# A row copy one exponential sooner, and products of constants in three further gaps of the FFN's first tiles

## The reference, cut to what matters

```python
scores = jnp.einsum('bhqd,bhkd->bhqk', q, k) * scale      # 16 heads of 16
attn = jax.nn.softmax(scores, axis=-1)
msa = jnp.einsum('bhqk,bhkd->bhqd', attn, v)
...
gate = fp4_linear(x, w_gate)                              # 256 -> 704
y = fp4_linear(x, w_up)
h = jax.nn.silu(gate) * y
return fp4_linear(h, w_down)                              # fp4_linear quantises x and w in blocks of 16
```

## Time and profile before

| | us |
|---|---|
| three runs: median (lowest to highest) | 1751.27 (1739.05 to 1756.83) |
| the profiled execution, its own time | 1747.05 |
| its span, first to last instruction | 1745.3 |
| TensorE busy in the span | 1568.2 |
| VectorE busy | 1328.9 |
| ScalarE busy | 889.5 |
| GpSimd busy | 285.7 |

### The profile page before, as it was taken

The page is one execution under the profiler, slowest core; times in us unless marked ns, Lnnn a source line. Parts: engine busy times, 40 slices in busy tenths (PEclk is TensorE's granted clock), DMA queues, the critical chain, the costliest instruction groups (busy, mean ns, idle before and its releaser), DMA issues.

```text
span 1745.3 us, 28266 instructions
## 1 busy us (share of the span) xinstructions
PE 1568.2 (90%) x10646; PEld 940.9 (54%) x10646; DVE 1328.9 (76%) x2565; ACT 889.5 (51%) x1358; POOL 285.7 (16%) x383
## 2 busy tenths in 40 slices
PE   5977899996599999899999979999997999999895
PEld 1757899995243335565333557533335654333564
DVE  3585565542499988888998889899888889997686
ACT  1213354442357776144777624477772356778312
POOL 0053223222200030301003130100223010000120
PEclk8988999998699999899999989999999999999998
DMA  3127878775222220004222000322200022210000
GB/s 135 49 73 208 246 242 258 244 244 163 58 42 38 38 74 1 1 8 87 34 39 68 14 1 1 79 38 38 68 26 1 1 61 47 38 29 2 1 0 25
DMA packets 80306, 123.07 MB, mean 71 GB/s; under 512 B 13657, under 2 KB 55898, under 8 KB 80170
## 3 DMA queue, kind: packets, MB, share of 16 engines
q1 hardware_dynamic: 70794, 93.46, 20.7%
q0 software_dynamic: 9376, 27.80, 5.5%
HBM read 76.84 MB, written 18.61 MB: 55 GB/s over the span
## 4 chain that ended last, share of the span: by engine, by line
PE 71%; DVE 17%; issue 6%; ACT 3%; DMA 2%; POOL 1%; SPq 1%; ACTq 0%; DVEq 0%; POOLq 0%
PE PS L1065 13%; PE PS L1018 13%; PE PS L1176 7%; PE PS L943 7%; PE PS L931 6%; PE PS L1051 6%; DVE MX L1581 6%; PE PS L1186 5%; PE PS L988 3%; PE PS L1002 2%; PE PS L881 2%; PE PS L1135 1%; PE PS L1212 1%; DMA Pb<-W 1%; PE PS L920 1%
## 5 line engine op out<-in xcount | busy, mean ns | idle before, releaser
L1581 DVE TENSOR_REDUCE MX<-PS 128x1 f32<-128x512 f32 x1024 | 636.5, 683 | 70.1 <-PE PS L1018 69.2
L748 ACT ACTIVATE Pb<-PS 128x1024 f32<-128x1024 f32 x512 | 518.9, 1026 | 180.0 <-PE PS L1051 179.4
L1018 PE MATMUL PS<-Ks,Qs 48*128 48x512 f32 x1024 | 389.8, 455 | 35.0 <-ACT MR L741 28.8
L1051 PE MATMUL PS<-Qs,Ks 50*128 50x512 f32 x1024 | 360.4, 452 | 0.0
L1065 PE MATMUL PS<-Pb,V 128*32 128x256 f32 x4096 | 320.5, 390 | 0.5
L1018 PEld LDWEIGHTS PS<-Ks,Qs 48*128 48x128 f32 x1024 | 161.9, 184 | 243.7 <-DVE MX L1581 133.7
L1065 PEld LDWEIGHTS PS<-Pb,V 128*32 128x32 f32 x4096 | 83.8, 108 | 162.0 <-ACT Pb L748 87.1
L1051 PEld LDWEIGHTS PS<-Qs,Ks 50*128 50x128 f32 x1024 | 143.5, 185 | 24.4 <-ACT Pb L748 19.8
L943 PE MATMUL PS<-Pb,OT 128*128 128x256 f32 x624 | 141.0, 379 | 0.0
L931 PE MATMUL PS<-Ks,Qs 128*128 128x256 f32 x936 | 127.6, 294 | 8.0 <-DVE Ks L1461 8.0
L931 PEld LDWEIGHTS PS<-Ks,Qs 128*128 128x128 f32 x936 | 119.8, 197 | 10.5 <-DVE Ks L1461 9.4
(11 more groups left out here) (288 smaller groups left out, 1959.6 us busy)
## 6 DMA issues: line engine op xcount, KB each, us to landing
Pb<-W SPq DMA_DIRECT2D x78, 512.0 KB
y_slot<-V SPq DMA_DIRECT2D x39, 256.0 KB
Qs<-Qh SPq DMA_DIRECT2D x128, 64.0 KB, 2.3
Ks<-Kh SPq DMA_DIRECT2D x120, 64.0 KB, 2.3
V<-b SPq DMA_DIRECT2D x39, 128.0 KB
XT<-x_mid POOLq DMA_DIRECT2D x4, 1024.0 KB
out<-Pb POOLq DMA_DIRECT2D x4, 1024.0 KB, 6.8
OT<-xT SPq DMA_DIRECT2D x2, 1024.0 KB, 6.4
```

What stands on the lines that cost most here:

```text
L748: F["ex"].inc(act.activation(weights_of(n), PS[:, 2 * (n % 2):2 * (n % 2) + 2, :], ACT.Exp, scale=0.25))
L1018: F["slp"].inc(pe.matmul(PS[:, slot_bank(i), :], Qs[rows, p % NB, t * P:(t + 1) * P], Ks[rows, p % NB, kh * HALF:(kh + 1) * HALF], start=T ...
L1051: ins = pe.matmul(PS[:, 2 * (n % 2) + a, :], Ks[rows, p % NB, kt * P:(kt + 1) * P], Qs[rows, p % NB, qh * HALF:(qh + 1) * HALF], start=Tru ...
L1581: F["sld"].inc(dve.tensor_reduce(MX[:, p % 2, a, t, kh:kh + 1], PS[:, slot_bank(i), :], AX.X, ALU.max))
```

## The change

`turn_step` gives one step less for every unit from 1 to 15, so each copy of rows stands behind the exponential ahead of the one where it stood. TensorE's order in attention stays as it was. In the FFN the 36 products of the identity become 42, and three further groups are put in: 4 after the turns of x's tiles 0 and 1, 12 after the turn of tile 2 (ahead of `gate_up(1)`), and 12 after `gate_up(1)` (ahead of the turn of `HQ(0)`). The three further groups write bank 7.

```diff
             if u + 1 == NU:
-                return LAST + 1
-            return next(n for n in range(NU * KT) if ahead_of(n + 1) > UN * (u + 1) + LATER)
+                return LAST
+            return next(n for n in range(NU * KT) if ahead_of(n + 1) > UN * (u + 1) + LATER) - 1
...
-                for _ in range(36):
-                    pe.matmul(PS[:, 3, 0:P], ident[:, :], ident[:, :], start=True, stop=True)
+                def identities(n, bank):
+
+                    for _ in range(n):
+                        pe.matmul(PS[:, bank, 0:P], ident[:, :], ident[:, :], start=True, stop=True)
+
+                identities(42, 3)
...
                 F["trp"].inc(x_tile_turn(1, 4, D))
+                identities(4, 7)
                 gate_up(0)
                 F["trp"].inc(x_tile_turn(2, 5, 0))
+                identities(12, 7)
...
                     if t:
                         down(t - 1)
+                    else:
+                        identities(12, 7)
```

## The result

The kernel after takes 1733.0 us (median of 17 runs, 1719.34 to 1765.63) and the kernel before, beside it, 1756.56 us (17 runs, 1739.05 to 1771.09). The ratio is 0.9909, with a 95% interval of 0.988 to 0.9939: faster by 0.6 to 1.2%. The ratio goes by the fast executions alone, those within 1.5% of the fastest of their kernel, so it is not the quotient of the two medians, 0.9866. Forecast were 1711 us and a range of 1702 to 1729. The sign is right. The size is 16.0 us by the ratio and 23.6 by the medians, where 38 to 40 were forecast. A result within 1% had been given 0.07. The profiled execution took 1728.35 us, 18.7 us less than that of before.

What follows compares the result with a forecast made beforehand. The prediction took TensorE, busy 1568.2 of 1745.3 us, as the bound, so its idle places count. Copy 32 us and constants 6 us off 1747.05 give 1709, or 1713 from the median; forecast 1711 us, range 1702 to 1729.

Steps and rivals of the forecast that it cites:

- The copy's mechanism: In attention, the copy of rows starts one exponential sooner, so TensorE's score product no longer waits for its slot.
- Its size: Attention's gain from the sooner copy: 0.67 us in each of 52 units, bounds 26 to 35 us, 32 us taken.
- second rival: In attention, VectorE's reduction soon holds the score product instead and half the gain is lost: 1725 us; chance 0.13.
- first rival: In attention, the copy waits for the turned product and holds ScalarE's exponential: slower, 1762 us; chance 0.06.
- The constants: In the FFN's head, added products keep TensorE's clock up, shortening each sequence's third gate_up to 4.74 us: 6 us taken.
- The sum: Whole kernel: 1747.05 - 32 - 6 = 1709 us; from the runs' median 1713; 1711 us taken.
- third rival: In the FFN's head, the clock falls despite the fill; the last twelve products run at 1.2 GHz: 1726 us; chance 0.11.

Runs made afterwards that it cites:

- after again: The changed kernel, unaltered, run for a second profile on chip 12: 1760.61 us, with no ratio on record.
- chip 15: Chip without stalls; there the unaltered kernels were run again: after 1697.99 us (ratio 0.9812), before 1732.02 us (1.0009).
- The two kernels made for this question: The kernel after with the copy sooner only in units 1 to 11: 1702.74 us (0.983); only from unit 12 on: 1722.25 us (0.9943).
- sixteen in a row on chip 11: The kernel before with all gathers for the next sequence moved behind the last unit's maxima: 1802.99 us, ratio 1.0294.

## Why the prediction was right and wrong

**The copy's mechanism: right.** The wait of L1018 for L741 (28.8 us) is gone in the kernels whose copies all stand sooner (1.3 us are left in after again), and in sequence 3 of chip 15 two units take 20.6 to 20.7 us, as forecast. The timeline of after on chip 15 shows the order that the prediction drew:

```profile
844.09 0.28 PE L1025 MATMUL PS<-ident,NMs 128*16 128x128 f32 x1
...
844.40 0.27 ACT L741 ACTIVATE MR<-PS 16x128 fp32r<-16x128 f32 x1 [0.18 <-PE PS L1025]
...
844.96 0.64 PE L1065 MATMUL PS<-Pb,V 128*32 128x256 f32 x8
845.07 1.02 ACT L748 ACTIVATE Pb<-PS 128x1024 f32<-128x1024 f32 x1 [0.40 <-PE PS L1051]
...
846.20 0.64 PE L1065 MATMUL PS<-Pb,V 128*32 128x256 f32 x8
```

The copy follows the turned product at once, its exponential has still 0.40 us of slack, and the weighings are 1.24 us apart where one interval was 2.00.

**Its size: right, where nothing else intervenes.** 32 us were taken; attention in the four sequences of chip 15 is shorter by 8.1, 8.1, 8.2 and 8.5, together 32.9 us. The groups by line there, of after:

```profile
L1589 DVE TENSOR_REDUCE MX<-PS 128x1 f32<-128x512 f32 x1024 | 635.9, 684 | 29.4 <-PE PS L1018 26.0
```

and of before:

```profile
L1581 DVE TENSOR_REDUCE MX<-PS 128x1 f32<-128x512 f32 x1024 | 637.5, 684 | 60.7 <-PE PS L1018 60.6
```

VectorE's idle time behind L1018 falls by 34.6 us, by as much as the forecast had it (69 to 35). VectorE didn't become the bound (second rival), and ScalarE's wait for the turned product costs nothing (first rival).

**The constants: right in place, conditional in size.** With the last twelve products the third `gate_up` is 4.74 us in all 44 sequences of the eleven profiles that have them. Between the first two profiles that is 6.1 us, as forecast. But the kernels without these products lose the time in only 13 of the 28 sequences of their seven profiles: in all four of the first one, in none of before on chip 15. In the other fifteen it is the second `gate_up` that is long (6.9 to 8.0 us), and there it costs nothing. So the four long ones of the first profile were chance, and lucky for the term, which over all seven would be 13 x 6.1 / 4 / 7 = 2.8 us an execution. It should have read "0 to 6, by whether the clock falls there in this execution"; the prediction's lower bound of 0 was for another reason, a fall in spite of the products.

**The sum: this is the step that failed.** "1747.05 - 32 - 6 = 1709" takes for granted that attention keeps all else as it is. Set against chip 15, attention in the first profile of before had lost 2.5, 3.0, 3.1 and -0.1 us to the stalls, 8.5 in all; in that of after it lost 9.4, 12.1, 10.1 and 0.1, 31.7 in all. The difference of 23.2 us is the missing term, which the sum put at nothing: some 20 are the 47.8 us at 1.2 GHz, and the other 3 aren't taken apart. The account of the two profiles closes: 32.9 - 23.2 from attention, 6.1 from the FFN's head, 3.8 from an earlier start of the first attention (486.35 for 490.19, which the change doesn't touch), -0.9 in the last sequence's end, together 18.7 of 18.7 us. So 3.8 of the profile's 18.7 us aren't the change's. The third rival named the clock but looked for it in the FFN's head, where the earlier fall had been seen.

What could have been read beforehand: the stalls stood in the profile of before; sequence 3's attention was 3 us shorter than the others; and runs that differ by 17 us (1739 to 1757) with a profile that shows no fall suggest that other executions lose something that this one doesn't.

**Open.** It stays open why all three engines stand still during a burst of gathers on one chip and not on another; no run here separates a path in the memory from something that GpSimd's own work holds. One more difference stands in the traces. The 64 gathers signal their landing 1024 times; the eight profiles of chip 15 have 1004 to 1024 of these signals on record, those of the sessions that stall have 299 to 485, and with spread gathers 868 and 897. So on those chips something also goes wrong with the signals or with their recording while gathers run, and it goes with the bursts; whether it is the cause isn't shown. Nor is it shown that the sooner copy makes a fall likelier. 9 of 9 sequences against 5 of 9 and the longer time at low clock are a hint; the size of the gap is none, since before has stalls of TensorE of 1.25 us without a fall. The two kernels made for this question met the chip without stalls.

## What to carry to other kernels

A profile is one execution on one chip. Before a sum rests on it, compare stages that do the same work (here four sequences): the difference shows what the environment takes, and that part may grow as the stage gets denser. Where the runs' spread is about as large as the expected gain, run before and after on the same chip more than once, and look at granted clocks even where the engine is busy throughout. Four indirect gathers in a row inside a stage bound by the engines are worth spreading: it costs 2 to 4 us on a quiet chip, and saves the kernel before 28 to 31 on one that stalls.

## What was unexpected of the hardware

- A burst of indirect gathers (DMA share 1.00 to 1.06, 385 GB/s) stalled TensorE, VectorE and ScalarE together for 1.2 to 1.9 us in the first session's profile of after, ScalarE for up to 11.6 us with sixteen in a row on chip 11, and none of them on chip 15, where the first of these programs ran at the same DMA share.
- After such a stall TensorE had 1.2 GHz for 13.7 to 20.5 us on end in the first profile of after, and for up to 82 us in that of the copy alone, although it was busy throughout, at a cost of 0.43 us for each. Gaps of 1.1 to 1.25 us were followed by a fall in some sequences and by none in others, with the same program.
- The kernel before thus has a median of 1731 us on one chip and 1766 us on another, a difference as large as the whole change.
